# A vision layer on one core: attention weights divided by their sum before the transpose, float32 value products with V stationary, and the cosine products on GpSimd

## The reference

```
h = haar_reconstruction(x)                                  # (32, 256, 256)
h = concatenate([cls_tok, h], axis=1)                        # 257 tokens of 256 features
q, k, v = split(einsum('bsd,dhf->bshf', layernorm(h), w_qkv) + b_qkv, 3)   # 16 heads of 64
q = q * cos + rotate_half(q) * sin
k = k * cos + rotate_half(k) * sin
scores = q k^T / sqrt(192) + alibi, causal
weights = softmax(scores)
attn = weights @ v
h = h + einsum('bshd,hdm->bsm', attn, w_out) + b_out
h = h + ffn(layernorm(h))                                    # 256 -> 1024 -> 256, quantised
```

## Time and profile before

| | us |
|---|---|
| median of 3 runs | 2415.41 |
| lowest, highest | 2415.02, 2421.36 |
| the profiled execution, its own time | 2422.74 |
| its span, first to last instruction | 2420.7 |
| PE busy, share of the span | 1851.4, 76% |
| DVE busy | 1731.4, 72% |
| ACT busy | 1359.0, 56% |
| POOL busy | 1023.0, 42% |
| mean granted TensorE clock, as a share of 2.4 GHz | 0.933 |

### The profile page before, as it was taken

The page is one execution under the profiler, slowest core; times in us unless marked ns, Lnnn a source line. Parts: engine busy times, 40 slices in busy tenths (PEclk is TensorE's granted clock), DMA queues, the critical chain, the costliest instruction groups (busy, mean ns, idle before and its releaser), DMA issues.

```text
span 2420.7 us, 54955 instructions
## 1 busy us (share of the span) xinstructions
PE 1851.4 (76%) x16742; PEld 1334.8 (55%) x16742; DVE 1731.4 (72%) x5024; ACT 1359.0 (56%) x3841; POOL 1023.0 (42%) x1098
## 2 busy tenths in 40 slices
PE   2667878777787887777878787778778787887775
PEld 2644555555555655555556555555555555555543
DVE  2536778778777677777767776877767677777775
ACT  0125666666656565655656656665655565666653
POOL 0136445444555344445544443455534344554400
PEclk6769999999999999999999999999999999999986
DMA  7312111111111111111111111111111111111100
GB/s 180 127 35 53 40 43 49 42 42 40 42 48 49 46 41 44 42 38 40 49 50 48 39 45 40 40 39 48 49 46 41 40 42 36 47 49 45 45 10 9
DMA packets 98170, 114.79 MB, mean 47 GB/s; under 512 B 22722, under 2 KB 60067, under 8 KB 97571
## 3 DMA queue, kind: packets, MB, share of 16 engines
q1 hardware_dynamic: 97826, 110.61, 17.6%
HBM read 26.62 MB, written 8.42 MB: 14 GB/s over the span
## 4 chain that ended last, share of the span: by engine, by line
PE 35%; DVE 29%; issue 20%; ACT 9%; POOL 3%; SPq 2%; DVEq 1%; ACTq 0%; DMA 0%; POOLq 0%
PE bank L624 16%; PE bank L774 4%; DVE arena L1055 3%; DVE ptr_l L1060 3%; DVE arena L1207 3%; DVE es L1210 3%; DVE th L1203 3%; PE bank L858 3%; PE bank L714 2%; PE bank L712 2%; PE bank L726 2%; ACT arena L509 2%; DVE ao L1079 2%; PE bank L735 1%; PE bank L658 1%
## 5 line engine op out<-in xcount | busy, mean ns | idle before, releaser
L480 POOL TENSOR_TENSOR rot<-rot,sin 128x512 f32<-128x512 f32 x256 | 331.0, 1293 | 1072.4 <-DMA rot<-rq 1072.2
L509 ACT ACTIVATE arena<-arena,nm 128x129 f32<-128x129 f32 (+1 forms) x1024 | 458.5, 457 | 65.0 <-DVE nm L1055 65.0
L1055 DVE CUSTOM_DVE_ANT_0 arena<-bank,bias 128x129 f32<-128x129 f32 (+1 forms) x1024 | 304.9, 354 | 174.1 <-PE bank L714 164.5
L624 PE MATMUL bank<-xt_h,weights 128*128 128x256 f16 x2048 | 398.1, 282 | 20.1 <-ACT rq L501 17.6
L624 PE MATMUL bank<-arena,ptr_h 128*128 128x64 f16 x3072 | 211.1, 196 | 258.1 <-DVE ptr_l L1060 161.1
L514 ACT ACTIVATE ptr_h<-bank 128x384 f16<-128x384 f32 x512 | 249.9, 488 | 231.4 <-PE bank L726 231.3
L501 ACT ACTIVATE rq<-bank,bqk 128x256 f32<-128x256 f32 x512 | 213.8, 469 | 275.6 <-PE bank L624 270.9
L484 POOL TENSOR_TENSOR arena<-arena,rot 128x256 f32<-128x256 f32 (+1 forms) x384 | 344.4, 911 | 30.3 <-POOL rot L480 0.5
L624 PEld LDWEIGHTS bank<-arena,ptr_h 128*128 128x128 f16 x3072 | 182.1, 100 | 305.8 <-DVE ptr_l L1060 226.8
L1060 DVE TENSOR_TENSOR ptr_l<-bank,ptr_h 128x384 f16<-128x384 f32 x512 | 281.5, 550 | 53.8 <-ACT ptr_h L514 53.7
L624 PE MATMUL bank<-xt_l,weights 128*128 128x256 f16 x1024 | 288.5, 282 | 0.0
(11 more groups left out here) (187 smaller groups left out, 3562.1 us busy)
## 6 DMA issues: line engine op xcount, KB each, us to landing
rot<-rq SPq DMA_DIRECT2D x1024, 64.0 KB, 2.0
arena<-in_x SPq DMA_DIRECT2D x4, 2048.0 KB, 18.2
xin<-in_x SPq DMA_DIRECT2D x32, 256.0 KB, 2.7
hr<-hr SPq DMA_DIRECT2D x32, 256.0 KB, 2.4
out<-h SPq DMA_DIRECT2D x64, 128.0 KB, 1.7
arena<-in_L_attn_w_qkv SPq DMA_DIRECT2D x2, 1536.0 KB, 6.5
arena<-in_L_attn_w_out SPq DMA_DIRECT2D x1, 1024.0 KB, 10.1
arena<-in_L_ffn_w_gate SPq DMA_DIRECT2D x1, 1024.0 KB, 6.4
```

The costliest lines, as they stand in the source:

```text
L480: pool.tensor_tensor(r, r, sin[:, :].unsqueeze(1).broadcast_to([P, 2, SIDE]), ALU.mult).then_inc(t2_ready, 1)
L509: act.activation(cols, cols, ACT.Exp, bias=nm[:, t, h:h + 1], scale=-1.0, accum_out=rs[:, t, h:h + 1]).then_inc(e_done, 1)
L624: ins = pe.matmul(dst, lhs[l], rhs[r], start=start and n == 0, stop=stop and n == len(parts) - 1)
L1055: dve.tensor_tensor_reduce(r[:, cols], bank[:, cols], b, -1.0, 3.0e38, ALU.add, ALU.min, nm[:, t, h:h + 1]).then_inc(t_done, 1)
```

## The change

- `normalise` now works on one head at a time and ahead of the transpose: DVE takes the reciprocal of the row sums of the head and multiplies its three 128x128 blocks of weights in place by two `tensor_scalar` instructions (128x128 and 128x2x128, float32, `tp` to `tp`). It stands in DVE's slot k for head k+1, right behind `ttr`. `ao` and the products after each four heads go.
- `transposes` waits for `n_done`; ACT copies the three transposed blocks to float32 `pt`, a ring of four (`turned_weights`). `pt_lo` goes.
- `values` works on two heads at a time, in even slots. V is one float32 tile `v` and is the stationary operand, 64 columns wide; the transposed weights are the moving one, 256 columns for the first key block and 128 for the second. The first head writes PSUM partitions 0 to 63, the second 64 to 127. The result is already transposed, so `out_transposes` goes.
- ACT and DVE split it into `at_h` and `at_l` from `o_bank` in the slots of `AT_SLOT` (5, 9, 13, and 1 of the next step). DVE's V remainder goes.
- `COS_ON_POOL` names all eight groups.
- `pt_use`, `at_use` go: the two transposition banks now serve the heads alone, one each in turn.

```diff
-COS_ON_POOL = [1, 3, 4, 6]
+COS_ON_POOL = list(range(8))
+RING = 4
+AT_SLOT = [5, 9, 13, 1]
...
-            def pt_hi(c, h, start):
-                if not start or h >= 2:
-                    act.wait_ge(pv_done, 16 * c + h - 1)
-                use = pt_use(h, start)
-                hi_of(c, use, ptr_h[:, h % 2], pt_bank[use % 2][:, 0:3 * P].rearrange("p (b n) -> p b n", b=3))
+            def turned_weights(c, h, start):
+                if not start or h >= RING:
+                    act.wait_ge(pv_done, 8 * c + h // 2 - 1)
+                act.wait_ge(pt_ready, 16 * c + h + 1)
+                act.activation(pt[:, h % RING, :, :], pt_bank[h % 2][:, 0:3 * P].rearrange("p (b n) -> p b n", b=3), ACT.Copy).then_inc(pt_done, 1)
...
+            def at_hi(c, g):
+                if g == 0 and not first(c):
                     act.wait_ge(op_ready, c)
+                act.wait_ge(pv_done, 8 * c + 2 * g + 2)
+                act.activation(at_h[:, :, 2 * g:2 * g + 2, :].rearrange("p t j n -> p j t n"), o_bank[:, :].rearrange("p (j t n) -> p j t n", j=2, t=T), ACT.Copy).then_inc(ath_done, 1)
...
             def transposes(c, h, start):
+                if not start or h >= 2:
+                    pe.wait_ge(pt_done, 16 * c + h - 1)
+                pe.wait_ge(n_done, 16 * c + h + 1)
                 r = tp[:, h % 4]
                 for n, col in enumerate((0, W0, W0 + P + 1)):
+                    ins = pe.transpose(pt_bank[h % 2][:, n * P:(n + 1) * P], r[:, col:col + P], eye[:, :])
                 ins.then_inc(pt_ready, 1)
...
+            def values(c, j, par, start):
+                pe.wait_ge(pt_done, 16 * c + 2 * j + 2)
+                if j == 0:
+                    pe.wait_ge(v_done, 4 * c + 4)
+                if j % 2 == 0 and (j >= 2 or not start):
+                    pe.wait_ge(atl_done, 4 * c + j // 2)
+                dst = o_bank[:, (j % 2) * SIDE:(j % 2 + 1) * SIDE]
+                for kb in range(2):
+                    for two in range(2):
+                        h = 2 * j + two
+                        lanes, feat = slice(two * DH, (two + 1) * DH), slice(h * DH, (h + 1) * DH)
+                        blocks = (0, 2) if kb == 0 else (2, 3)
+                        ins = pe.matmul(dst[lanes, kb * P:SIDE], v[par][:, kb, feat], pt[:, h % RING, blocks[0]:blocks[1], :].rearrange("p b n -> p (b n)"),
+                                        start=kb == 0, stop=kb == 1)
                 ins.then_inc(pv_done, 1)
...
-                    if has_c and k >= 1:
-                        values(c, k - 1, cp, start)
+                    if has_c and k >= 2 and k % 2 == 0:
+                        values(c, k // 2 - 1, cp, start)
...
-            def pt_lo(c, h, start):
-                use = pt_use(h, start)
-                lo_of(c, use, ptr_l[:, h % 2], pt_bank[use % 2][:, 0:3 * P].rearrange("p (b n) -> p b n", b=3), ptr_h[:, h % 2])
...
+            def normalise(c, h):
+                dve.wait_ge(e_done, 32 * c + 2 * h + 2)
+                r = tp[:, h % 4]
+                late = r[:, W0:W0 + 2 * (P + 1)].rearrange("p (b n) -> p b n", b=2)[:, :, 0:P]
+                inverse = rinv[:, :, h % 2]
+                dve.reciprocal(inverse, rs[:, :, h]).then_inc(rinv_ready, 1)
+                dve.wait_ge(rinv_ready, 16 * c + h + 1)
+                ts(r[:, 0:P], r[:, 0:P], inverse[:, 0:1], None, ALU.mult)
+                ts(late, late, inverse[:, 1:2], None, ALU.mult).then_inc(n_done, 1)
+
+            def at_lo(c, g):
+                dve.wait_ge(ath_done, 4 * c + g + 1)
+                lo, hi = (at[:, :, 2 * g:2 * g + 2, :].rearrange("p t j n -> p j t n") for at in (at_l, at_h))
+                tt(lo, o_bank[:, :].rearrange("p (j t n) -> p j t n", j=2, t=T), hi, ALU.subtract).then_inc(atl_done, 1)
...
+                    if k < HEADS - 1 and has_c:
+                        normalise(c, k + 1)
+                    if k == HEADS - 1 and next_c(s):
+                        normalise(s, 0)
...
-                    if has_b and k in V_SLOT:
-                        v = V_SLOT.index(k)
-                        cols = slice(v % 2 * 512, (v % 2 + 1) * 512)
-                        dve.wait_ge(vh_done, 4 * s + v + 1)
-                        stt(vl[par][:, v // 2, cols], b_bank[:, :], 1.0 / WSCALE, vh[par][:, v // 2, cols], ALU.mult, ALU.subtract).then_inc(vl_done, 1)
```

More of the change, by code:

```diff
@@ L88, in link @@
         self.settle()
-def pt_use(h, start):
-    return h if start and h < 3 else h + (h - 3) // 4
-def at_use(g, last=False):
-    return 19 if last else 5 * g + 7
+AT_SLOT = [5, 9, 13, 1]
 def vit_layer(nc, x, cls_tok, Wa, ba, Wd1, bd1, Wd2, bd2, Wd3, bd3, w_qkv, b_qkv, w_out, b_out,
@@ L570, in step @@
                         exps(*ahead[:2])
-                    if k == 2 and has_e and not start:
-                        at_hi(c - 1, 3, not has_c)
-                    if has_c and k >= 6 and k % 4 == 2:
-                        at_hi(c, k // 4 - 1)
+                    if k in AT_SLOT:
+                        if k == AT_SLOT[3]:
+                            if has_e and not start:
+                                at_hi(c - 1, 3)
+                        elif has_c:
+                            at_hi(c, AT_SLOT.index(k))
                     if has_e and k == XQ_SLOT + 1:
@@ L738, in values @@
-            def values(c, h, par, start):
-                pe.wait_ge(pt_free, 20 * c + pt_use(h, start) + 1)
-                if h == 0:
-                    pe.wait_ge(vl_done, 4 * c + 4)
-                if h % 4 == 0 and (h > 0 or not start):
-                    pe.wait_ge(ao_ready, 4 * c + h // 4)
-                feat = slice(h * DH, (h + 1) * DH)
-                for t in range(T):
-                    dst = o_bank[:, t * SIDE + (h % 4) * DH:t * SIDE + (h % 4 + 1) * DH]
-                    blocks = [(0, 0)] if t == 0 else [(1, 0), (2, 1)]
-                    for n, (pb, kb) in enumerate(blocks):
-                        ins = split3(dst, (ptr_h[:, h % 2, pb, :], ptr_l[:, h % 2, pb, :]),
-                                     (vh[par][:, kb, feat], vl[par][:, kb, feat]), n == 0, n == len(blocks) - 1)
+            def values(c, j, par, start):
[12 more added lines that the diff above has]
+                                        start=kb == 0, stop=kb == 1)
@@ L847, in step @@
                             ins.then_inc(ready, 1)
-                    if k == 2 and has_e and not start:
-                        out_transposes(c - 1, 3, not has_c)
-                    if has_c and k >= 6 and k % 4 == 2:
-                        out_transposes(c, k // 4 - 1)
                     if has_e and k in DOWN_SLOT:
@@ L1176, in step @@
                         ins.then_inc(t1_done, 1)
-                    if has_c:
-                        pt_lo(c, k, start)
-                    if has_c and k >= 4 and k % 4 == 0:
-                        normalise(c, k // 4 - 1)
-                    if has_e and not start and k == 0:
-                        normalise(c - 1, 3)
                     if has_a and k == SYN_SLOT:
@@ L1192, in step @@
                         assert ca.n == CHAIN_A, ca.n
-                    if k == 2 and has_e and not start:
-                        at_lo(c - 1, 3, not has_c)
-                    if has_c and k >= 6 and k % 4 == 2:
-                        at_lo(c, k // 4 - 1)
+                    if k in AT_SLOT:
+                        if k == AT_SLOT[3]:
+                            if has_e and not start:
+                                at_lo(c - 1, 3)
+                        elif has_c:
+                            at_lo(c, AT_SLOT.index(k))
                     if has_e and k in GU_SLOT:
```

84 lines of the change are left out of this document (22 added, 62 removed).

## The result

| | before | changed |
|---|---|---|
| median, us | 2421.15 (20 runs) | 2399.08 (20 runs) |
| lowest, highest | 2408.34, 4532.66 | 2380.87, 2425.01 |
| ratio, 95% interval | | 0.9904 [0.9881, 0.9928] |
| span of the profiled execution | 2420.7 | 2405.2 |
| DVE busy | 1731.4 | 1629.7 |

A forecast was written before the change was run, and what follows sets the result against it. PE and DVE were taken as two queues in step, each leading half a period. Per image -0.6 - 1.5 - 1.3 (DVE's half) + 1.5 = -1.9 us, 61 us over 32, from 2422.7 to 2360 us; range 2215 to 2500, forecast's own 2290 to 2405.

The forecast's parts named there:

- the new wait for `at_lo` in slot 6: PE in slot 6: the wait behind the quantisation replaces the 0.81 us wait for `ptr_l`; counted at nothing.
- PE's own work, -0.6: PE: new value products cost 6.9 us an image, old products (5.6) and `ao` transposes (1.9) go; net -0.6, bounds -2.2 and +3.1.
- The rival with serial column halves: PE's value products: column halves run one behind the other, +3.1 us an image instead of -0.6; 2420 us, up to 2480; chance 0.11.
- the holding of 9.9 us an image: DVE's division products in POOL's stretch: POOL holds them 0.9 us a head for 11 heads, 9.9 us an image.
- The free price of 0.75 us: DVE's division without POOL's hold: reciprocal, two products and semaphore take 0.75 us a head, 12.0 us an image.
- The quantisation, +1.5: Quantisation of the tokens: waits for `rstd2` behind one more 1.27 us cosine product on POOL; +1.5 us an image, bounds 0 and +3.
- PE's waits, -1.5: PE ahead of the value products: half of the 3.0 us an image waiting for `ao` goes; -1.5, bounds 0 and -8.1.
- a whole slot to spare: The new guard of `o_bank`: ACT's and DVE's split, one slot behind the last product, has this slack in slots 9, 13 and 1.
- the halved wait for `ao`: PE's wait for `ao`, 3.0 us an image, counted by half for the part of the period PE leads: -1.5 us.
- At nothing: the clock: PE's clock was 0.97 to 1.00 of 2.4 GHz in the period read, so no gain was counted.
- The rival "POOL holds DVE longer": DVE's division products: each waits 0.94 us on POOL instead of 0.45, 7.0 us an image at heads 6 to 12; 2585 us; chance 0.27.
- "The queues come apart": PE's value products: all 258 us of waiting go, 6.6 us an image more than counted; 2150 us, half gives 2255; chance 0.17.

The follow-up runs named there:

- The pause: Changed kernel with one more wait on POOL: behind `rstd2` it goes on only when DVE has finished the scales of the quantisation; 2343.0 us, ratio 0.9667.

## Why the prediction was off

The direction held, and 2399 lies inside the range and just inside the forecast's own one of 2290 to 2405. The size did not hold: 22 us instead of 61. The step that failed is the new wait for `at_lo` in slot 6: it was priced at the 0.81 us of the wait that it replaced, and it is 3.1 us, since the held quantisation stands in front of it.

- **PE's own work, -0.6: right.** A pair of heads goes from start to start in 0.81 us (values at 1204.90, next matmul at 1205.71); 0.86 was priced. PE's busy time went up by 42.5 us all the same, from 1851.4 to 1893.9; the clock loss rose by 24 us, and since a busy time counts modelled ends, the rest decides nothing. The rival with serial column halves (1.32) is dead, and on this the trace agrees with the rule of the Trainium skill (TensorE: Matmul & The Clock Gate, Part 3, Packing small matmuls) that was cited.
- **DVE, the holding of 9.9 us an image: three times too large, and put in the wrong place.** The new products are held 0.066 + 0.138 = 0.2 us a head (means of 351 and 479 ns, minima of 285 and 341), 3.3 us an image. The size of one hold was near: between 300 and 2250 us 181 of the 920 products are held, 0.50 us each, and 0.45 was taken. Their number was not: 22 an image were taken, and it is 6. The free price of 0.75 us was right. DVE's busy time fell by 101.7 / 32 = 3.2 us an image; I had it rise by 2.7. The 1.17 us of the earlier trace rows belongs to the quantisation and stayed there; why the products of the division meet POOL so seldom while it is busy half of the time was not tried.
- **The quantisation, +1.5, bounds 0 and +3: the step that failed.** In the image shown it is 0.8 us longer, so the term itself looks small. Its reason did not come, though: 1.27 of the 1.5 us was the cosine product in front of `rstd2`, and POOL stood idle there 31 times, 103.7 us in all, waiting for DVE; the 0.8 us are more hold inside. And I priced only how much later it ends. Of its 5.73 us in the kernel before 3.2 were hold already (a free one takes 2.53), and the change put the guard of `o_bank` behind all of it.
- **PE's waits, -1.5: failed with it.** I wrote that in slot 6 the wait for `at_lo` "takes its place", at 0.81 us. It is 3.1 us in 28 images, and in 17 of them the clock falls behind it. The slack of "a whole slot to spare" held for slots 13 and 1. It did not hold for slot 9, where `at_lo` stands behind `xn` and PE waits 1.2 us for it in slot 10 of every image; with groups 5 and 7 on DVE that grows to 3.3 us. Of the halved wait for `ao` nothing was left: 258 us of idle time became 272. What PE did win is its wait for V's remainder, 69.6 us, now 2.1, and that for `xq`, 48.6 us, now 16.5.
- **At nothing: the clock.** I read 0.97 to 1.00 in one period and gave it nothing. Over 1950 us the clock loss rose by 24 us, which is more than half of the 39 us that are missing, if each us of it counted; how much of it did isn't shown.
- **Not in the sum: the wait at the loop's turn.** It fell from 35.6 to 11.3 us in the profiled executions. If it counted in full, the terms that I did price gave nothing at all.
- **The rival "POOL holds DVE longer".** Its mechanism was right, its place and price were not: 0.2 us a head where it wanted 1.17. The same lock on the quantisation is worth 2.4%, so without it the changed kernel is at 2343, and the 2360 forecast was near a kernel in which nothing holds the quantisation. That nearness is luck in part, since the sum had other terms wrong by as much.
- **"The queues come apart" did not come.** Every product has a slot more, but PE and DVE meet in slots 5 to 7 and again in slot 10 of every image, and what is gained elsewhere is waited away there. The pause takes most of the first meeting away, and 1.6% appears.

## What to carry to other kernels

When a change moves a wait, look at what stands in front of the new releaser in its queue, and price the wait by the length of all of that, with its holds, not by the wait that it replaces. A chain of small dependent products on DVE should not run beside an engine that holds it: 2.7 us of standing still on POOL bought 4.0 us on DVE and 2.4% of the time here, but only 0.6 to 0.8% in the kernel before, where PE waited 0.81 us behind that chain. If moving work between two places only changes which wait is long (139 us for `at_lo` or 128 us for `xq`), look for the cause ahead of both. And an edit can move a wait that it was not aimed at, as the one at the loop's turn: compare every row of waits before a gain is put down to a part of the change.

## What the runs showed of the hardware

- POOL's hold does not spread evenly over DVE's instructions. A product from SBUF to SBUF whose start falls just behind the start of POOL's paid nearly a whole instruction of POOL, whatever its own size: 1.18 us for 128x2 elements. The reduction in the same chain (L1057) was never held: it started at 1240.23, POOL's instruction at 1240.19, and it took 0.69 us, as it does with POOL standing still, and 685 to 687 ns in all 33 images. Most products of the division pay nothing: the median of 512 products of 128x128 is 287 ns against a minimum of 285 and a maximum of 1399 ns. The Trainium skill (SBUF — State Buffer, Who interferes with whom) has the exclusive lock; the trace agrees with it, at 1244.06 against 1244.04 us.
- A gap of PE of 2.8 us was followed by 1.55 us instead of 0.87 for the same eight matmuls; of 28 gaps of 2.8 to 3.7 us, 17 were followed by a lower clock within 4 us and 11 were not. Filling a gap of 3.7 us with unused matmuls took the clock loss from 205 to 73 us and the time down by 3.2%. Four kernels that differ only in the order of DVE's instructions have mean clocks from 0.878 to 0.92 and times from 2399 to 2505 us.
